# Post-norm transformer layer: output projection over two steps, transposes and a value phase in one step, maxima combined by a reduction

## The reference, cut to what matters

```python
# x: (16, 1024, 256); 16 heads of 16; scale = 16 ** -0.5
q = rope(x @ Wq.T + bq) * scale;  k = rope(x @ Wk.T + bk);  v = x @ Wv.T + bv
attn = softmax(q @ k.T)                        # per head, 1024 x 1024
x = layernorm(x + (attn @ v) @ Wo.T + bo)
h = relu(x @ quantize(W1).T + b1)              # ternary weights, 256 -> 1024
x = layernorm(x + h @ quantize(W2).T + b2)     # 1024 -> 256
```

## Time and profile before

| | |
|---|---|
| median of 3 runs | 3572.74 us (3565.26 to 3574.76) |
| the profiled execution's own time | 3569.3 us |
| its span | 3567.5 us |
| PE busy | 3397.2 us, 95% |
| PE weight loads | 1824.1 us, 51% |
| DVE busy | 3025.8 us, 85% |
| ACT busy | 2502.4 us, 70% |
| POOL busy | 2072.8 us, 58% |
| mean granted TensorE clock | 0.972 of full |

### The profile page before, as it was taken

One profiled execution on the slowest core, in us unless ns is written; L12 is line 12 of the kernel. 1 busy time (PEld: TensorE's weight loads), 2 busy tenths in 40 slices (PEclk: granted clock), 3 DMA queues, 4 the chain that ended last, 5 costly groups with the idle time before them and its releaser, 6 DMA issues.

```text
span 3567.5 us, 80272 instructions
## 1 busy us (share of the span) xinstructions
PE 3397.2 (95%) x30726; PEld 1824.1 (51%) x30726; DVE 3025.8 (85%) x5671; ACT 2502.4 (70%) x4884; POOL 2072.8 (58%) x2088
## 2 busy tenths in 40 slices
PE   4899999999999999999999999999999999999975
PEld 3443555555555555555555555555555555544444
DVE  4788899999999999999999999999999999988611
ACT  2177777777777777777777777777777777777740
POOL 2143666666666666666666666666666666634346
PEclk9599999999999999999999999999999999999977
DMA  5344454445345534443444345434543453444110
GB/s 144 48 102 93 93 116 94 92 105 116 91 92 109 114 90 94 109 107 93 97 111 101 99 98 110 100 97 95 116 95 88 107 116 91 89 87 80 33 40 25
DMA packets 292288, 336.92 MB, mean 94 GB/s; under 512 B 59712, under 2 KB 241856, under 8 KB 291648
## 3 DMA queue, kind: packets, MB, share of 16 engines
q1 hardware_dynamic: 291904, 331.79, 41.2%
HBM read 193.27 MB, written 138.41 MB: 93 GB/s over the span
## 4 chain that ended last, share of the span: by engine, by line
PE 88%; DVE 4%; ACT 2%; issue 2%; POOL 2%; DMA 1%; SPq 0%; DVEq 0%; POOLq 0%; ACTq 0%
PE sc L623 28%; PE ob L640 27%; PE job L501 23%; PE ms L612 9%; ACT prob L745 2%; DVE mx L867 1%; DVE mxp L861 1%; DVE mxp L1023 1%; POOL hid_r L1086 1%; PE ms L501 0%; PE ob L501 0%; POOL ka L1163 0%; DMA qa<-qk_parts 0%; DVE mxt L876 0%; POOL xt_r L1064 0%
## 5 line engine op out<-in xcount | busy, mean ns | idle before, releaser
L861 DVE TENSOR_REDUCE mxp<-ms 128x1 f32<-128x512 f32 x4032 | 2583.2, 681 | 308.5 <-PE ms L612 269.8
L745 ACT ACTIVATE prob<-sc 128x512 f32<-128x512 f32 x4096 | 2229.8, 599 | 787.6 <-PE sc L623 758.3
L623 PE MATMUL sc<-qa,ka 50*128 50x512 f32 x4096 | 1581.4, 446 | 44.6 <-ACT prob L745 38.4
L612 PE MATMUL ms<-ka,qa 48*128 48x512 f32 x4032 | 1577.9, 449 | 7.9 <-DVE mxp L861 3.1
L623 PEld LDWEIGHTS sc<-qa,ka 50*128 50x128 f32 x4096 | 682.5, 185 | 1174.3 <-ACT prob L745 1014.0
L640 PE MATMUL ob<-prob,v_sb 128*17 128x512 f32 x8192 | 1086.3, 602 | 1.1 <-ACT at_st L751 0.5
L612 PEld LDWEIGHTS ms<-ka,qa 48*128 48x128 f32 x4032 | 676.5, 185 | 36.2 <-DVE mxp L861 33.9
L1084 POOL CAST hid_r<-hid 128x512 fp32r<-128x512 f32 x256 | 156.8, 613 | 415.1 <-DVE hid L917 268.9
L1086 POOL TENSOR_TENSOR hid_r<-hid,hid_r 128x512 fp32r<-128x512 f32 x256 | 328.1, 1282 | 20.5
L1075 POOL TENSOR_TENSOR ve<-mv,eps_sb 128x2 f32<-128x2 f32 x128 | 25.0, 196 | 484.4 <-DVE mv L896 484.4
L501 PE MATMUL job<-h_t,w_sb 64*128 64x256 f32 x3840 | 283.8, 280 | 0.0
(11 more groups left out here) (99 smaller groups left out, 2764.7 us busy)
## 6 DMA issues: line engine op xcount, KB each, us to landing
qk_parts<-parts SPq DMA_DIRECT2D x128, 512.0 KB, 4.2
ka<-qk_parts SPq DMA_DIRECT2D x384, 128.0 KB, 4.7
qa<-qk_parts SPq DMA_DIRECT2D x384, 128.0 KB, 7.6
attention<-at_st SPq DMA_DIRECT2D x128, 256.0 KB, 4.0
v_ones<-v_st SPq DMA_DIRECT2D x64, 272.0 KB, 3.3
v_sb<-v_ones SPq DMA_DIRECT2D x64, 272.0 KB, 9.1
xt_sb<-xt SPq DMA_DIRECT2D x64, 256.0 KB, 7.5
xn<-x SPq DMA_DIRECT2D x64, 256.0 KB, 7.3
```

The lines of the kernel that those rows point to most:

```text
L612: nc.tensor.matmul(ms[upto(b, g, NS1, at) % MS_BANKS][:, :], operand(qa, b, g, j, ROWS)[:, qt * P:(qt + 1) * P], operand(ka, b, g, j, ROWS ...
L623: nc.tensor.matmul(sc[upto(b, g, HG * STEPS, n) % SC_BANKS][:, :], operand(ka, b, g, j, ROWS + MROWS)[:, tt * P:(tt + 1) * P], operand(qa, ...
L745: nc.scalar.activation(prob[st_ % 2][:, j, :], sc[upto(b, g, HG * STEPS, n) % SC_BANKS][:, :], ACT.Exp).then_inc(s["exp_done"], 1)
L861: nc.vector.reduce_max(mxp[(b * G + g) % 2][:, kh, j * TT + qt:j * TT + qt + 1], ms[upto(b, g, NS1, at) % MS_BANKS][:, :], AX.X).then_inc( ...
```

## The change

`t3` becomes `t3a` (step 0) and `t3b` (step 1), each after part 1, and t4 moves from step 5 to 6. In units with one projection e0, e1, o0, o1 move one step later, and v0 stays at step 6, beside t4: a step may now have two jobs, tail first. The value phases write columns 256 to 511 of the job banks; v0 doesn't wait for the emptying of t4's columns, it raises a semaphore of its own (`v_half`) for v1, and ACT waits for that too before it copies t4's result. DVE's tables move; `combine` is one `reduce_max` over 128x32x2. On POOL `rotate_even` comes ahead of the first norm's end, `rotate_odd` (two products) ahead of `split_first_norm`, the four sums are a function of their own, `add_products`, behind it, and `sum_x` moves between the second and third `split_hidden`.

```diff
-PROJ_JOBS = {1: [{1: "e0", 2: "e1", 3: "o0", 4: "o1", 6: "v0", 7: "v1"}],
+PROJ_JOBS = {1: [{2: "e0", 3: "e1", 4: "o0", 5: "o1", 6: "v0", 7: "v1"}],
-TAIL_JOBS = {0: "t3", 5: "t4", 8: "f0", ...
+TAIL_JOBS = {0: "t3a", 1: "t3b", 6: "t4", 8: "f0", ...
-RECIP_AT = (11, 3)
-FIRST_NORM = {(0, 3): "sums", (1, 2): "stats 0", (2, 0): "stats 1", (2, 2): "moments 0"}
-SECOND_NORM = {(0, 0): "stats 0", (0, 2): "stats 1", (1, 0): "moments 0"}
+RECIP_AT = (12, 3)
+FIRST_NORM = {(1, 1): "sum 0", (1, 2): "sum 1", (2, 2): "stats 0", (4, 0): "stats 1", (4, 2): "moments 0"}
+SECOND_SUMS = {(15, 1): "sum 0", (15, 2): "sum 1"}
+SECOND_NORM = {(0, 1): "stats 0", (0, 3): "stats 1", (2, 0): "moments 0"}
...
-def job_at(b, g, step, tail):
+def jobs_at(b, g, step, tail):
     found = projected(b, g)
...
+    jobs = [("tail", (b - 1, g), TAIL_JOBS[step])] if tail and step in TAIL_JOBS else []
+    return jobs + [("proj", at, table[step]) for at, table in zip(found, PROJ_JOBS.get(len(found), [])) if step in table]
...
             tt(oc[:, :, :], od_sb[:, :, :], cos, ALU.mult).then_inc(s["products"], 1)
+
+        def add_products(wait, engine, b, g):
+
+            tt = engine.tensor_tensor
             wait.wait_ge(s["products"], upto(b, g, 4, 4))
...
                 if phase == 1 and first:
-                    pe.wait_ge(s["halves_done"], halves[0])
+                    if tell:
+                        pe.wait_ge(s[tell[0]], tell[1])
+                    else:
+                        pe.wait_ge(s["halves_done"], halves[0])
...
+                for what, n in bank_free:
+
+                    if not (kind == "v" and phase == 0 and what == "t4_taken"):
                         wait_used(pe, s[what], n)
...
-                last = in_halves([bank[:, 0:TQ] for bank in job], terms, phase)
+                columns = slice(TQ, 2 * TQ) if kind == "v" else slice(0, TQ)
+                last = in_halves([bank[:, columns] for bank in job], terms, phase,
+                                 tell=("v_half", upto(b, g, 1, 1)) if kind == "v" else None)
...
                         for j in range(HG):
                             scores(b, g, st_, j, tiles[j])
-                            if job_:
-                                free = run(job_, j, free)
-                            if j == (3 if job_ else 1):
+                            if j == 1:
+                                for job_ in jobs:
+                                    free = run(job_, free)
+                            if j == (3 if jobs else 1):
                                 weigh_before(b, g, st_, first)
...
                     act.wait_ge(s["t4_ready"], upto(b, g, 1, 1))
+                    for at in projected(b + 1, g):
+                        act.wait_ge(s["v_half"], upto(*at, 1, 1))
...
-                nc.vector.tensor_tensor(mx[:, :], mxp[(b * G + g) % 2][:, 0, :], mxp[(b * G + g) % 2][:, 1, :], ALU.max).then_inc(s["max_done"], 1)
+                nc.vector.reduce_max(mx[:, :], mxp[(b * G + g) % 2][:, :, :].rearrange("p k n -> p n k"), AX.X).then_inc(s["max_done"], 1)
...
+                for at in proj[:1]:
+                    rotate_even(pool, nc.gpsimd, *at)
                 if tail:
                     finish_first_norm(b - 1, g)
                     sum_h1(b - 1, g)
                 for at in proj[:1]:
-                    rotate_even(pool, nc.gpsimd, *at)
+                    rotate_odd(pool, nc.gpsimd, *at)
                 if tail:
                     split_first_norm(b - 1, g)
                 for at in proj[:1]:
-                    rotate_odd(pool, nc.gpsimd, *at)
+                    add_products(pool, nc.gpsimd, *at)
...
                 if tail:
-                    for n in range(FT // 2):
-                        split_hidden(b - 1, g, n)
+                    split_hidden(b - 1, g, 0)
+                    split_hidden(b - 1, g, 1)
+                if prepared(b, g)[0] >= 0:
+                    sum_x(*prepared(b, g))
+                if tail:
+                    split_hidden(b - 1, g, 2)
+                    split_hidden(b - 1, g, 3)
```

More of the change, by code:

```diff
@@ L490, in _, with in_halves @@
             halves = [0]
-            def in_halves(banks, terms, phase, first=True, last=True):
+            def in_halves(banks, terms, phase, first=True, last=True, tell=None):
                 if phase == 1 and first:
-                    pe.wait_ge(s["halves_done"], halves[0])
+                    if tell:
+                        pe.wait_ge(s[tell[0]], tell[1])
+                    else:
+                        pe.wait_ge(s["halves_done"], halves[0])
                 for n, pair in enumerate(terms):
@@ L504, in in_halves @@
                 if phase == 0 and last:
-                    halves[0] += 1
-                    done.then_inc(s["halves_done"], 1)
+                    if tell:
+                        done.then_inc(s[tell[0]], 1)
+                    else:
+                        halves[0] += 1
+                        done.then_inc(s["halves_done"], 1)
                 return done
             def proj_job(b, g, kind, phase, bank_free):
[L511 to L514, removed]
+                if phase == 0 and kind == "e":
+                    pe.wait_ge(s["xt_low"], upto(b, g, 1, 1))
+                for what, n in bank_free:
+                    if not (kind == "v" and phase == 0 and what == "t4_taken"):
                         wait_used(pe, s[what], n)
@@ L649, in weigh_before, with run @@
                     weigh(b + (g - 1) // G, (g - 1) % G, STEPS - 1)
-            def run(job_, place, free):
+            def run(job_, free):
                 stage, at, name = job_
                 if stage == "proj":
-                    return proj_job(*at, name[0], int(name[1]), free) if place == 1 else free
+                    return proj_job(*at, name[0], int(name[1]), free)
                 if name[0] == "g":
                     part = int(name[1])
-                    return second_layer(*at, part // 2, range(part % 2 * FT // 2, (part % 2 + 1) * FT // 2), free) if place == 1 else free
+                    return second_layer(*at, part // 2, range(part % 2 * FT // 2, (part % 2 + 1) * FT // 2), free)
                 if name[0] == "f":
[L660 to L663, removed]
+                    return first_layer(*at, int(name[1]) // 2, int(name[1]) % 2, free)
+                return tail_job(*at, name, int(name == "t3b"), free)
             def batch(b, tail=True, last=False, first=False):
@@ L670, in batch @@
                     for st_ in range(STEPS):
-                        job_ = job_at(b, g, st_, tail)
+                        jobs = jobs_at(b, g, st_, tail)
                         tiles = [maximum_tiles(b, g, 4 * st_ + n, last) for n in range(4)]
@@ L765, in proj_job @@
                             v_st[:, :, tl, :, 0:HD],
-                            job[tl][:, 0:D].rearrange("p (g h c) -> p g h c", g=G, h=HG), ACT.Copy)
+                            job[tl][:, TQ:TQ + D].rearrange("p (g h c) -> p g h c", g=G, h=HG), ACT.Copy)
                     done.then_inc(s["v_taken"], len(tiles))
@@ L805, in batch @@
                             take_outputs(b + (g - 1) // G, (g - 1) % G, 1)
-                        job_ = job_at(b, g, st_, tail)
                         exps(b, g, st_, 0)
                         exps(b, g, st_, 1)
-                        if job_:
+                        for job_ in jobs_at(b, g, st_, tail):
                             finish(job_)
@@ L902, in take_key_half @@
                     wait_used(dve, s["v_stored"], upto(b, g, 16, 0))
[L903 removed]
+                    nc.vector.tensor_copy(v_st[:, :, 1, :, 0:HD], job[1][:, TQ:TQ + D].rearrange("p (g h c) -> p g h c", g=G, h=HG)
                                           ).then_inc(s["v_taken"], 1)
@@ L933, in first_norm @@
                 if step is None:
[L934 to L937, removed]
                     return
@@ L974, in batch @@
                                 invert(*prepared(b, g))
[L975 to L978, removed]
+                            if tail:
+                                second_norm(b - 1, g, SECOND_SUMS.get((st_, part)))
+                            for stage, at, name in jobs_at(b, g, st_, tail) if part == 1 else []:
+                                if stage == "proj":
                                     take_key_half(*at, name)
-                                elif part == 1 and name in ("f1", "f3"):
+                                elif name in ("f1", "f3"):
                                     for p in range(2):
                                         take_hidden(*at, int(name[1]) - 1 + p, job[1][:, p * TQ:(p + 1) * TQ])
-                                elif part == 2 and name == "g3":
-                                    second_norm(*at, "sum 0")
-                                    second_norm(*at, "sum 1")
             nc.vector.memset(ob[:, :], 0.0).then_inc(s["ob_zero"], 1)
@@ L1000, in _ @@
                 rotate_odd(dve, nc.vector, 0, g)
```

(1 more changed line is left out.)

18 lines of the change are left out of this document (6 added, 12 removed).

## The result

The changed kernel takes 3532.35 us, the median of four runs (3529.33 to 3535.46), against 3569.0 for the kernel before beside it: the ratio is 0.990 (95% interval 0.9875 to 0.9924), 37 us or 1.0% faster. The forecast was 3543, faster, with a range of 3500 to 3562. The profiled execution spans 3530.8 us, against 3567.5.

A forecast was written before the change was run, and what follows sets the result against it. An ordinary step was bound by a 3.10 us circle through TensorE and ACT, so only longer steps could shrink. From 3569.3: -51 +10 -24 +38 = -27, 3542, plus 1 for the median: 3543 us; own range 3530 to 3555, eight-in-ten 3500 to 3562.

The forecast's parts named there:

- Step 0: TensorE, 60 units with a tail: t3's second phase moves to a covered place, 3.95 to 3.10 us, 51 us saved.
- Its lower end: If DVE did bind in the steps after the change, 0.4 us of the 0.85 us a unit would come back.
- t4 with v0: Step 6, 54 units: transposes plus first value phase last 1.29 us, 0.18 beyond the known cover, costing 10 us.
- The norm on POOL: From step 4: POOL finishes the norm 6.4 us after step 4's start, t4 needs it at 6.8; cost nothing.
- The long `mx`: Combining of maxima on DVE: the one-operand reduction no longer waits for POOL's product; 38 units times 0.63, 24 us saved.
- Where the stall goes: Step 8: POOL's later products three and four hold up `high` and `low`, 0.70 us in 54 units, 38 us lost.
- `low` alone: Step 8: if only `low` waits, it comes just behind product four's start at 3.35 us, and the end is the same.
- the rival's 3505: Step 8: no new stall, POOL's timing differs or DVE slips in ahead; the 38 us fall away, 3505 us; chance 0.22.
- POOL keeps the way: Step 8: a DVE instruction arriving mid-product is passed over by the queued product; 77 us instead of 38, 3581; chance 0.08.
- The rule of the Trainium skill: DVE against POOL: tensor_reduce never contends; two-SBUF-input instructions and two-port tensor_scalar do, the loser waiting for the whole instruction.
- The last six units: The six units not having both a tail and a projection merely hold t4 one step later, without the pair's 0.18 us.

The follow-up runs named there:

- the four profiles named above: Profiles of the kernel before (3569.0 us), the changed kernel twice (3532.35, 3528.7 us), and that kernel with `high` and `low` moved behind part 1 of step 9 (3499.2 us).

## Why the prediction was right, step by step

- **Step 0.** Right in place and size: -51 us forecast, -52 measured, and with the phase put back the 52 come back in the trace (47 by the medians). That a job of 1.03 us after scores 1 is free was read off a job of 1.11 us. Its lower end (DVE holds the step) is excluded.
- **t4 with v0.** Mis-sized: +10 us forecast, +2 measured. The step that failed is the addition of 0.41 and 0.88: v0's first matmul starts 0.21 us behind t4's first (1901.46 and 1901.67 below), so the pair is over in 1.16 us instead of 1.29, and step 6 grew by 0.04 us where the sum had 0.18.

```profile
1901.46 0.41 PE L558 MATMUL job<-id_sb,h 64*128 64x64 f32 x8
...
1901.67 0.95 PE L505 MATMUL job<-wv_r,xt_r 64*128 64x256 f32 x12
```

- **The norm on POOL.** Right: the moments reach POOL 3.0 us into step 4 (1897.73 against a step start at 1894.72), the normalised h is ready at 1900.93 and the transposes' weight loads start at 1901.23. They don't wait, with 0.3 us of cover where 0.4 were forecast.
- **The long `mx`.** Right: -24 us forecast, and alone in the kernel before it gives 24.
- **Where the stall goes.** Right: products three and four at 2.2 and 3.4 us after step 8's start, forecast 2.1 and 3.3; the first reduction of step 9 3.46 us after the combining, forecast 3.46; 0.70 us a unit, forecast 0.70. Net of the stall removed, steps 9 and 10 gave +17 us where the sum had +14. Wrong was the remark in it that `low` alone would end the same: it gets in ahead of product four (3497 us, near the rival's 3505).
- **POOL keeps the way** (0.08): excluded. The combining that came in mid-product was let in ahead of the next product.
- **The rule of the Trainium skill.** What the Trainium skill's page "SBUF — State Buffer" ("Who interferes with whom") states in three parts, the runs now bear out in all three: the reduction doesn't wait (208 to 225 ns over 64), the form with two SBUF operands does (0.75 us), and so does the tensor_scalar (0.85 us), which the kernel before could not show.
- **The last six units.** Not in the sum, and rightly: t3b and t4 only move there. Steps 2 and 7 become 2.83 us, but steps 1 and 6, which were 3.04 and 2.83, become 3.18 and 3.09: about 0.1 us a unit, under 1 us in all.

The forecast lay 11 us above the median. Against the profiled execution it is 10 too high: 8 from the pair, 1 from step 0, 3 the other way from the stall, and 4 from the rest, in which the clock of the first unit and of two late steps has the largest part. The error in the stall works against the others, so the total is a little nearer than its terms.

## What to carry to other kernels

When a stall on a shared resource is removed by moving work of the other engine, work out where both stand afterwards: the busy stretch that is moved will meet the next instruction of the same kind, and here that gave back 38 of the 75 us that the two good parts of the change had won. A job is free in a step if a circle through another engine is the longer one there; read its size from the longest job that is already hidden, and read the length of two jobs in a row from their starts, not by adding durations. And an experiment that adds work in one place can come out at zero because it shifts a collision elsewhere, so look at both steps before saying that the work was hidden.

## What the runs showed of the hardware

A DVE tensor_scalar of only 32 elements a partition (0.17 us by itself), with one SBUF operand, lasts up to 1.25 us beside a POOL tensor_tensor of 1.3 us and 1.61 us beside one of 2.37 us, while a reduction of the same tile, beside the same product, takes 0.18. The waiting DVE instruction goes in when the product in progress ends, even where POOL has the next one ready, so that in these 54 units no wait is longer than one product (the longest `high` is 1.27 us, in the version with the old combining); one that comes 0.08 us behind the start of a product waits for the whole of it. `low` could also start 0.1 us ahead of the end of product three without a longer duration (1893.41, and the product ends at 1893.53); no run shows why.

The granted clock isn't the same in all stretches of these kernels. From 230 to 3100 us of the profiles before and after it is 1.00; over the first unit its mean lies between 0.63 and 0.85 in the four profiles named above, with a step of 7.49 us at 0.50, and two late steps before ran at 0.79 and 0.76. What decides whether the first unit is spent at the lower level, no run shows.
